# Second cross attention: earlier additions and gathers; fp4 codes of the last self attention loaded during it

## What is computed

```python
x = x + L0_xattn(layernorm(x), ctx)      # 16 heads, 8 kv heads
x = x + L0_attn(layernorm(x))
x = x + L0_ffn(layernorm(x))             # 64 experts, 8 of them per row, CAP = 64
x = x + L1_xattn(layernorm(x), ctx)      # 16 heads, RMS norm of q and k
x = x + L1_attn(layernorm(x))            # weights = codes * scales, one scale per block of 32 rows
x = x + L1_ffn(layernorm(x))             # 8 dense experts, top 2
```

```python
pos = (jnp.cumsum(onehot, axis=0) * onehot).sum(-1) - 1
dest = jnp.where(pos < CAP, slot_expert * CAP + pos, E * CAP)
slot_out = yb[dest] * topk_w[...]        # eight rows of yb for each row of x, added up
```

## Time and profile before

| | |
|---|---|
| median of 3 runs | 3096.58 us (3093.29 to 3100.2) |
| the profiled execution | 3071.94 us |
| span in its trace | 3070.2 us, mean TensorE clock 0.96 |
| TensorE busy | 2809.2 us (91%) |
| VectorE, ScalarE, GpSimd | 48%, 44%, 24% |
| second cross attention | about 1343 to 2146 us, iteration 1 from 1488 to 1588 |
| last self attention | from 2147 us |

### The profile page before, as it was taken

One profiled execution on the slowest core, in us unless ns is written; L12 is line 12 of the kernel. 1 busy time (PEld: TensorE's weight loads), 2 busy tenths in 40 slices (PEclk: granted clock), 3 DMA queues, 4 the chain that ended last, 5 costly groups with the idle time before them and its releaser, 6 DMA issues. The chain is left out here.

```text
span 3070.2 us, 50984 instructions
## 1 busy us (share of the span) xinstructions
PE 2809.2 (91%) x13964; PEld 2100.9 (68%) x13964; DVE 1478.7 (48%) x4967; ACT 1352.0 (44%) x4875; POOL 741.9 (24%) x948
## 2 busy tenths in 40 slices
PE   6999999798999999878898889889499999997999
PEld 5888888686444444455666566657378888886887
DVE  3665555575777444446543554354033333332433
ACT  2555445465666666535443443344122322221333
POOL 1333222264555100134224322430400000000000
PEclk8999999899999999999999999999699999998999
DMA  4001000201600244125335543452910000000000
GB/s 153 27 26 28 21 21 15 86 0 47 249 2 1 75 121 119 38 70 128 87 75 83 106 94 75 77 106 64 220 29 0 0 0 0 0 0 28 11 7 10
DMA packets 190904, 176.26 MB, mean 57 GB/s; under 512 B 32347, under 2 KB 171032, under 8 KB 189106
## 3 DMA queue, kind: packets, MB, share of 16 engines
q1 hardware_dynamic: 167762, 143.95, 16.7%
q0 software_dynamic: 14592, 27.33, 5.9%
q10 hardware_dynamic: 8416, 3.57, 0.9%
HBM read 147.41 MB, written 39.90 MB: 61 GB/s over the span
## 5 line engine op out<-in xcount | busy, mean ns | idle before, releaser
L491 PE MATMUL xa_score_ps<-cross_ctxT,xa_qT 128*128 128x257 f32 (+1 forms) x1024 | 328.2, 408 | 28.5 <-DVE xa_shift L735 21.0
L511 PE MATMUL xa_mix_ps<-xa_probsT,xa_keys 128*128 128x256 f32 x1024 | 319.7, 396 | 26.6 <-POOL xa_keys L872 26.6
L216 PE MATMUL rt_kn_key_ps<-moe_w_wk,cross_ctxT 128*128 128x512 f32 x560 | 248.7, 597 | 0.8 <-DVE moe_kn_stats L265 0.4
L498 PE MATMUL xa_probsT_ps<-all_ident,xa_probs 128*128 128x128 f32 x1024 | 208.6, 287 | 38.3 <-DVE xa_probs L747 22.5
L619 ACT ACTIVATE xa_probs<-xa_probs,xa_shift,xa_row_scale 128x257 f32<-128x257 f32 x256 | 153.8, 601 | 203.8 <-DVE xa_shift L735 200.0
L478 PE MATMUL xa_misc_ps<-xa_xnT,cross_folded 128*128 128x256 f32 x1024 | 234.4, 383 | 6.2 <-ACT xa_squares L604 5.6
L511 PEld LDWEIGHTS xa_mix_ps<-xa_probsT,xa_keys 128*128 128x128 f32 x1024 | 198.3, 200 | 55.9 <-POOL xa_keys L872 29.4
L627 ACT ACTIVATE xa_probsT<-xa_probsT_ps 128x256 f32<-128x256 f32 x512 | 187.7, 368 | 102.5 <-PE xa_probsT_ps L498 102.0
L520 PE MATMUL xa_misc_ps<-cross_folded,xa_mixT 128*128 128x256 f32 x1024 | 228.2, 379 | 0.0
L478 PEld LDWEIGHTS xa_misc_ps<-xa_xnT,cross_folded 128*128 128x128 f32 x1024 | 195.9, 192 | 40.1 <-ACT xa_squares L604 12.2
L498 PEld LDWEIGHTS xa_probsT_ps<-all_ident,xa_probs 128*128 128x128 f32 x1024 | 135.6, 147 | 124.2 <-DVE xa_probs L747 74.4
(11 more groups left out here) (309 smaller groups left out, 5289.2 us busy)
## 6 DMA issues: line engine op xcount, KB each, us to landing
xa_key_scale<-rk SPq DMA_DIRECT2D x256, 128.5 KB
ctx_cols<-cross_ctxT SPq DMA_DIRECT2D x8, 1028.0 KB, 12.4
cross_ctxT<-ctx_cols SPq DMA_DIRECT2D x64, 128.5 KB, 2.4
xa_rows<-in_ctx_dram SPq DMA_DIRECT2D x64, 128.0 KB, 2.2
xa_last_key<-in_ctx_dram SPq DMA_DIRECT2D x128, 64.0 KB, 2.9
xa_keys<-in_ctx_dram SPq DMA_DIRECT2D x64, 128.0 KB, 2.3
cross_folded<-in_L_ffn_w_gate_dram SPq DMA_DIRECT2D x32, 192.0 KB, 2.5
cross_folded<-in_L_ffn_w_up_dram SPq DMA_DIRECT2D x32, 192.0 KB, 2.7
```

Of the source, the lines that this page charges most:

```text
L216: pe.matmul(self.key_ps[m % self.banks][0:n, :], self.ctxT[:, c * P:c * P + n], self.wk[:, q * 512:(q + 1) * 512], start=True, stop=True). ...
L491: pe.matmul(score_ps[s % 2][:, 0:S2], qT[:, b, r * HR:(r + 1) * HR, :].rearrange("p h t -> p (h t)"), columns[:, b % RING, :] if layer els ...
L498: ins = pe.transpose(probsT_ps[s % 2][:, k * P:(k + 1) * P], probs[:, s % SR, k * P:(k + 1) * P], ident[:, :])
L511: ins = pe.matmul(mix_ps[b % 2][:, cols], keys[:, b % RING, k, :], probsT[:, b % 2, k, cols], start=(k == 0), stop=(k == KB - 1))
```

## The change

In the second cross attention the sixteen takes are made two per step in steps 0 to 7, the places and the four portions of gathers stand behind items 3 to 6, all rows of the first tile ahead of the second's (the takes alternate between the tiles), row statistics at step 12, `normalize` at 16 and `norm_scale` at item 4. The first iteration's takes need their rows sooner: eight of the gathers are made in `bridge`, and the prologue's sixteen become eight. The columns get memory of their own. `ctxT` becomes `big`, which lives to the last self attention: while the second cross attention runs, SP loads wq, wk and wv codes of one group (three loads of 512 KB) after each of its iterations 0 to 3 into `big`, and ahead of its last iteration the scales of the first four pieces (16 loads of 128 KB) into `spare`, which is qT's memory in layer 0 and wq's in layer 1. The wo codes (their memory holds the gathered rows until then) and the scales of pieces 4 to 15 are loaded in the last self attention. `last_cols` keeps 64 columns in layer 0 (one more copy), and a copy and two waits for it go.

Nothing is changed in the amount of multiplication or in the number of rows gathered for an iteration. The core of the diff:

```diff
+SA_WEIGHT = NC * H * HD
+SA_GROUPS = 4
+SCALE_SLOTS = 4
...
         LOADS = 48 if layer else 32
-        ROW_STATS = ST // 2 if layer == 0 else ST // 2 + R
+        FIRST_GATHER = 3
+        ROW_STATS = ST // 2 if layer == 0 else ST // 2 - R
...
-            GOT = G * K0 * D
-            got = ctxT[:, 0:GOT].rearrange("p (g k d) -> p g k d", g=G, k=K0)
-            columns = ctxT[:, GOT:GOT + RING * S2].rearrange("p (r s) -> p r s", r=RING)
+            got, columns = next_rows(ctxT), sc.sb("columns", [P, RING, S2])
+            codes_ahead, scales_ahead = sc.sem("codes_ahead"), sc.sem("scales_ahead")
...
-            sp.wait_ge(last_ready, 1)
-            with sp.Fori(0, ITERS) as i:
+            def items(i):
...
+            for g in range(SA_GROUPS):
+                items(g)
+                for name in ("wq", "wk", "wv"):
+                    after.load_codes(sp, name, g, codes_ahead)
+            with sp.Fori(SA_GROUPS, ITERS - 1) as i:
+                items(i)
+            sp.wait_ge(n_made, ITERS * (G * NQ))
+            for m in range(SCALE_SLOTS):
+                after.load_scales(sp, m, scales_ahead)
+            items(ITERS - 1)
+            sp.wait_ge(codes_ahead, 16 * 3 * SA_GROUPS)
+            sp.wait_ge(scales_ahead, 16 * SCALE_SLOTS * (P // FP4_ROWS))
...
-                    dve.wait_ge(gathered, (i + 1) * (16 * G * K0))
+                    dve.wait_ge(gathered, i * (16 * G * K0) + 16 * K0)
...
-                    if layer == 1 and not last and R <= s < R + G * K0:
-                        take(i, s - R)
+                    if layer == 1 and not last and s < G * K0 // 2:
+                        take(i, 2 * s)
+                        take(i, 2 * s + 1)
...
+                dve.tensor_copy(last_cols[:, :], score_ps[0][:, 0:B])
...
                         norm_scale(i + 1, link)
-                    if layer == 1 and not last and b >= NB // 2:
-                        if b == NB // 2:
+                    if layer == 1 and not last and FIRST_GATHER <= b < FIRST_GATHER + 4:
+                        if b == FIRST_GATHER:
                             next_places(i + 2)
-                        gather(b - NB // 2)
+                        gather(b - FIRST_GATHER)
                 if layer == 1 and not last:
-                    pool.wait_ge(gathered, (i + 2) * (16 * G * K0))
+                    pool.wait_ge(gathered, i * (16 * G * K0) + 16 * K0 * (1 + G))
                     row_scales(i + 1, link)
...
             def gather(quarter):
                 for n in range(quarter * K0 // 2, (quarter + 1) * K0 // 2):
-                    t, k = n % G, n // G
+                    t, k = n // K0, n % K0
...
                 next_places(1)
-                pool.wait_ge(last_ready, 1)
-                gather(0)
-                gather(1)
-                pool.wait_ge(gathered, 8 * G * K0)
+                gather(2)
+                gather(3)
+                pool.wait_ge(gathered, 16 * K0)
             if layer == 0:
                 pool.memset(ones[:, :], 1.0).then_inc(ones_set, 1)
                 pool.wait_ge(pre_loaded, 16)
             if layer == 1:
                 row_scales(0, link)
-                gather(2)
-                gather(3)
...
+def next_rows(ctxT):
+    return ctxT[:, 3 * SA_WEIGHT:3 * SA_WEIGHT + 2 * K0 * D].rearrange("p (g k d) -> p g k d", g=2, k=K0)
...
-            for t in range(G):
+            for t in range(G + 1):
+                to = got[:, t] if t < G else next_rows(ctxT)[:, 0]
                 apart(pool, passed)
                 for k in range(K0):
-                    pool.indirect_dma_start(out=got[:, t, k, :], out_offset=None, in_=slot_out,
+                    pool.indirect_dma_start(out=to[:, k, :], out_offset=None, in_=slot_out,
                                             in_offset=bass.IndirectOffsetOnAxis(ap=slots_all[:, t, k:k + 1], axis=0),
                                             bounds_check=SLOTS, oob_is_err=False).then_inc(gathered[t], 16)
+            pool.wait_ge(gathered[G], 16 * K0)
...
+    def load_codes(self, sp, name, g, loaded):
+        chunks, cols = self.place(name, g)
+        sp.dma_start(self.piece(name, g), self.I[f"L1_attn_{name}_codes"].rearrange("(c p) n -> p c n", p=P)[:, chunks, cols]
+                     ).then_inc(loaded, 16)
+    def load_scales(self, sp, m, loaded):
+        PARTS = P // FP4_ROWS
+        name, g = self.pieces[m]
+        chunks, cols = self.place(name, g)
+        rows = self.I[f"L1_attn_{name}_scales"].rearrange("(c b) n -> b c n", b=PARTS)
+        for b in range(PARTS):
+            sp.dma_start(self.scale_slot(m)[b * FP4_ROWS:(b + 1) * FP4_ROWS, :, :],
+                         rows[b][chunks, cols].partition_broadcast(FP4_ROWS)).then_inc(loaded, 16)
...
-            PARTS = P // FP4_ROWS
-            for m, (name, g) in enumerate(pieces):
-                to, chunks, cols = piece(name, g)
-                if m >= 4:
-                    sp.wait_ge(scaled, m - 3)
-                sp.dma_start(to, I[f"L1_attn_{name}_codes"].rearrange("(c p) n -> p c n", p=P)[:, chunks, cols]
-                             ).then_inc(codes_loaded[m % 4], 16)
-                rows = I[f"L1_attn_{name}_scales"].rearrange("(c b) n -> b c n", b=PARTS)
-                for b in range(PARTS):
-                    sp.dma_start(scale_slot(name, m)[b * FP4_ROWS:(b + 1) * FP4_ROWS, :, :],
-                                 rows[b][chunks, cols].partition_broadcast(FP4_ROWS)).then_inc(codes_loaded[m % 4], 16)
+            for g in range(NG):
+                weights.load_codes(sp, "wo", g, codes_loaded)
+            for m in range(SCALE_SLOTS, len(pieces)):
+                sp.wait_ge(scaled, m - SCALE_SLOTS + 1)
+                weights.load_scales(sp, m, scales_loaded[m % SCALE_SLOTS])
...
-                to = piece(name, g)[0]
-                pool.wait_ge(codes_loaded[m % 4], 16 * (1 + P // FP4_ROWS) * (m // 4 + 1))
-                pool.tensor_tensor(to, to, scale_slot(name, m), ALU.mult).then_inc(scaled, 1)
+                to = weights.piece(name, g)
+                if m >= SCALE_SLOTS:
+                    pool.wait_ge(scales_loaded[m % SCALE_SLOTS], 16 * (P // FP4_ROWS) * (m // SCALE_SLOTS))
+                if name == "wo":
+                    pool.wait_ge(codes_loaded, 16 * NG)
+                pool.tensor_tensor(to, to, weights.scale_slot(m), ALU.mult).then_inc(scaled, 1)
...
+        big, spare = sc.sb("big", [P, KEYS]), sc.sb("spare", [P, NC * H * HD])
+        last_cols = sc.sb("last_cols", [P, B])
+        sa1 = fp4_weights(I, big, spare)
```

More of the change, by code:

```diff
@@ L1791, in bridge @@
             "gain_ready", "turned", "wT_ready", "multiplied", "folded_kept"))
-        gathered = [sc.pool_dma_sem(f"gathered{u}") for u in range(G)]
+        gathered = [sc.pool_dma_sem(f"gathered{u}") for u in range(G + 1)]
         passed, added = sc.sem("passed"), [sc.sem(f"added{u}") for u in range(G)]
@@ L1940, in routed_experts, with __init__, whole, place @@
             experts(nc, I, ident, slot_rows, slot_out, norms_of, w_in, w_out, part_in)
-        bridge(nc, I, x_sb, ident, slots_all, weights_all, slot_out, wk, wv, wo, gains, norms_of, folded, wq)
-def self_attention_fp4(nc, I, x_sb, ident, ahead):
+        bridge(nc, I, x_sb, ident, ctxT, slots_all, weights_all, slot_out, wk, wv, wo, gains, norms_of, folded, wq)
+class fp4_weights:
+    def __init__(self, I, big, spare):
+        self.I = I
+        self.wq, self.wk, self.wv, self.wo = (big[:, n * SA_WEIGHT:(n + 1) * SA_WEIGHT] for n in range(4))
+        self.scales = spare[:, :].rearrange("p (m c n) -> p m c n", m=SCALE_SLOTS, c=NC)
+        self.pieces = [(n, g) for g in range(SA_GROUPS) for n in ("wq", "wk")] + [(n, g) for n in ("wv", "wo") for g in range(SA_GROUPS)]
+    def whole(self, name):
+        flat = {"wq": self.wq, "wk": self.wk, "wv": self.wv, "wo": self.wo}[name]
+        return flat.rearrange("p (c n) -> p c n", c=H if name == "wo" else NC)
+    def place(self, name, g):
+        W = H * HD // SA_GROUPS
+        return (slice(g * H // SA_GROUPS, (g + 1) * H // SA_GROUPS), slice(0, D)) if name == "wo" else (slice(0, NC), slice(g * W, (g + 1) * W))
+    def piece(self, name, g):
+        chunks, cols = self.place(name, g)
+        return self.whole(name)[:, chunks, cols]
+    def scale_slot(self, m):
+        s = self.scales[:, m % SCALE_SLOTS, :, :]
+        return s.rearrange("p c n -> p (c n)").rearrange("p (h n) -> p h n", n=D) if self.pieces[m][0] == "wo" else s
+    def load_codes(self, sp, name, g, loaded):
[5 more added lines that the diff above has]
+        name, g = self.pieces[m]
+        chunks, cols = self.place(name, g)
+        rows = self.I[f"L1_attn_{name}_scales"].rearrange("(c b) n -> b c n", b=PARTS)
+        for b in range(PARTS):
+            sp.dma_start(self.scale_slot(m)[b * FP4_ROWS:(b + 1) * FP4_ROWS, :, :],
+                         rows[b][chunks, cols].partition_broadcast(FP4_ROWS)).then_inc(loaded, 16)
```

(6 more changed lines are left out.)

49 lines of the change are left out of this document (22 added, 27 removed).

## The result

| | before | changed |
|---|---|---|
| median (runs) | 3094.93 us (6) | 3115.83 us (6) |
| lowest, highest | 3086.01, 3102.19 | 3113.32, 3121.0 |
| second comparison, with the experiments | 3073.67 us (11) | 3089.45 us (6) |

The changed kernel is slower: ratio 1.007, interval 1.005 to 1.009; in the second comparison 1.0059, 1.0043 to 1.0074. The forecast said slower, by 28 us; measured are 20.9 and 15.8.

The account below looks back on a forecast made before the run. TensorE, 91% busy, was taken as the bound, leaving little to win outside its waits. 48 - 3 - 17 = +28 us gave 3100 profiled, median 3125; own range 3098 to 3150 (0.52), 8 in 10 from 3040 to 3165.

Parts of the forecast that it names:

- Takes: Second cross attention, steps 0 to 7: twelve more takes cost 3.7 us per iteration, bounds 0 and 5.6.
- Steps 8 to 31: Second cross attention: without waits, low clock and twelve takes, 31.0 us instead of 39.1; 4.4 won net of takes, without contention.
- Gathers beside loads: Second cross attention, items 5 to 7: loads sharing DMA engines with gathers cost 12.4 us per iteration, bounds 0 and 24.
- the signs of being wrong: Iterations of 96 us without key_scale waits, a granted clock falling in steps 8 to 31 (unpriced), or codes delaying the next iteration.
- Net of an iteration: Second cross attention: -4.4 + 12.4 = +8.0 us, +48 over iterations 1 to 6; iteration 0 -3; the last neither.
- Start of the last self attention: Fewer loads there let its loop start 14.4 us earlier, and no low clock follows: -17 us, bounds 0 and -34.
- the low clock's term: Start of the last self attention: without the wait for wo pieces no low clock follows, 2.6 us won.
- Codes ahead: Second cross attention: codes loads after iterations 0 to 3 cost 0, bound +12; scales ahead of the last 0, bound +6.
- Bridge: Eight more gathers in the bridge, eight fewer in the prologue: 10 us of GpSimd beside matmuls, cost 0, bound +5.
- The rule on taking turns between queues: DMA engines alternate queues packet by packet: 24 us for one item's key scales, +98 in sum, 3194; chance 0.04.

Follow-up runs that it names:

- the skip: Changed kernel, but the second cross attention's gathers skip choices without a place and the routing sets their weights to zero; 2984.66 us, ratio 0.9717 to the kernel before.
- codes late: Changed kernel without codes loads in the second cross attention; all codes load in the last self attention, four pieces' scales stay ahead; 3114.24 us, ratio 1.0139 to before.
- codes only: Changed kernel with takes, statistics and gathers put back where they were before; codes, scales and bridge stay as changed; 3028.96 us, ratio 0.9853 to before.
- skip and tail: Changed kernel skipping choices without a place, with tiles 16 and 17 also marked so; ratio to before 0.9865 (third group), 0.9689 (fourth group, 2975.3 us).

## Why the prediction was right, and where it was off

**The sign and the mechanism** held. The gathers beside loads that steps wait for are what makes the change slower; the waits for the keys and for `rstd` went as described; the loads of items 5 to 7 are the late ones; the last iteration is untouched. That the sum came out near is partly luck, though: the cross attention lost 61.9 us instead of 45 and the last self attention won 38.1 instead of 17. The steps one by one:

*Takes.* 3.7 us in steps 0 to 7. In the kernel with the skip these take 15.0 us (from 1481.68 to the share of step 8 at 1496.69), against 11.6: +3.4. Held.

*Steps 8 to 31*, reckoned at the last iteration's pace of 5.0 us an item. They can be faster: from 1496.69 to the norms at 1524.59 are 27.9 us, not 31.0. The pace of the last iteration was no floor. So the early order gives 8.5 us an iteration (92.0 against 100.5 on the mean of 1 to 5), not 4.4.

*Gathers beside loads*, 12.4 us between bounds of 0 and 24. Iterations 1 to 5 of the changed kernel are 20.3 us longer than with the skip (112.3 against 92.0). This is the term that was mis-sized: near the upper bound, and near the 22.0 us of DMA time that the gathers take. My choice assumed that half of it would find idle engines or drain behind the steps, but the DMA share in the stretch is 0.95. The row that gave the price was among those read: seven loads of an item took 14.5 us beside gathers. In iteration 1 the sets of seven now take 5.0 us (from 1508.08), 10.3 (from 1513.15, what I had worked out for one item with a portion) and 15.4, and VectorE waits 4.4, 7.4 and 6.7 us where I had charged 2, 5 and 5.4. The loss also has a part that I listed among the signs of being wrong and didn't price. Behind the stalls the clock is lower, 0.89 over the iteration against 0.98 with the skip, and TensorE's busy time for the same work is 90.6 against 84.0 us: 6.7 of the 19.6 us between these two iterations; in the other 12.9 it is idle.

*Net of an iteration* +8.0 was forecast, measured +11.8 in iterations 1 to 5, +4.3 in iteration 0 (forecast -3) and +0.3 in iteration 6 (forecast +8). Iteration 6 took 105.7 us before because of the 8.1 us wait for the keys behind GpSimd's pause, which I hadn't seen; the change removes that wait and puts the late loads in its place. In sum +63 instead of +45.

*Start of the last self attention*, -17. Measured -38, beyond the bound of -34, which had named the case of biases that land earlier. The step that failed is to let the chain begin at 2189.34: I kept the landing time of a DMA from a stage whose loads were about to change. It landed 26 us earlier against the stage's start. The amount of loads in the whole stage isn't the reason: in "codes late" 14 of the 16 MB are still loaded there, and the biases are first used 11.4 us after TensorE's first instruction (10.7 in the changed kernel).

What differs is what is issued first; that this decides the landing is argued, no run changes it alone. The kernel before issues whole pieces of 1 MB from the start, and its load of the output bias takes 14.8 us to issue on ScalarE's queue; in "codes late" only four loads of 512 KB are issued in the first 8 us, and it takes 3.4, as against 1.9 in the changed kernel.

One reading of that sum was also wrong: the 6.35 us behind the wait are two groups of sixteen matmuls, and 3.77 is the busy time of the first. Later pairs start 3.6 us apart, so the low clock's term is 2.8 instead of 2.6, which changes nothing.

*Codes ahead* 0: true for "codes only", at most 9.7 us beside the early gathers, within the bound of 12. *Bridge* 0: held, once the remote waits were told apart.

*The rule on taking turns between queues* would have given 24 us for one item's key scales, the same per iteration, and +98 in all. Waits for one item never reached 24 us (15.6 at most), and the sum was 77 us too high; it also charged iteration 6 and came with my small gains for the early order and the last self attention. The 20.3 us per iteration are near 24, but that doesn't bear the rule out: they are three items' waits and a lower clock, and whatever makes the waited loads stand behind all of the gathers would come near the gathers' own 22.0 us. The Trainium skill ("DMA: Bandwidth & Descriptors", section "Queues, rings and completion order") has the engines take turns packet by packet. With the profile's packets this trace doesn't agree: between 1530 and 1539 us, while the key scales of 8.96 us were issued and the engines were 93% busy, 561 packets of the plain loads went beside 235 of the gathers, 2.4 to one. Whether the profile's packets are those of the rule, no run shows.

What remains open: what the remote waits are, what GpSimd waits for in the pause of iteration 6, and how much of the 20.3 us would be left if the waits came without the lower clock, since no run held the one and changed the other.

## What to carry to other kernels

Before moving a transfer earlier, count what it takes of the DMA engines' time from the queue's own row, not its bytes, and charge all of it if the loads beside it are waited for and the engines are near full. A gather whose indices mostly name one row is a transfer of its own kind: drop these indices (out of bounds, with a weight of zero) or spread them; here that turned a loss of 0.6% into a gain of 3%, while the same skip gave nothing in the order that had hidden the gathers. And when loads leave a stage, don't keep the landing times of the ones that stay. Last, if one iteration of a loop is longer than the others, look for what is different in its rows before giving it their price.

## What the runs showed of the hardware

An indirect gather of 16 x 128 rows of 1 KB took 22.0 us of all 16 DMA engines when all read the same row and 8.9 us when they read distinct rows, with nearly the same packet count (768 and 774). When all its indices are out of bounds, packets still stand in the queue's row, 832 in 93 us of iteration 2, but they move 0.01 MB in 0.6% of that time (0.6 us):

```profile
q0 software_dynamic: 832, 0.01, 0.6%
```

In three profiles, with waits named remote, the program reaches the second cross attention 19 to 31 us later, and kernels differ in how much they lose: the ratio of the kernel with skip and tail is 0.9865 with these waits and 0.9689 without. A ratio is safe only between kernels that ran side by side.
